# A graph layer's finished rows: two columns of edges written by SP row by row instead of by two indirect DMAs of GpSimd

## What is computed

```python
proj = einsum('ni,rio->nro', x, relation_weight)      # 10 relations
att  = sum(proj[src, etype] * tanh(proj[dst, etype] + efeat), -1)
a    = softmax of att over the edges of one dst
h_nb = segment_sum(x[src] * a[:, None], dst)
out  = leaky_relu((x + h_nb) @ W1.T, 0.01) + leaky_relu((x * h_nb) @ W2.T, 0.01)
result = layernorm(x + out)                            # over the 64 features
```

## Time and profile before

| | us |
|---|---|
| median of 3 runs (lowest to highest) | 926.07 (923.43 to 927.35) |
| span of the profiled execution, first to last instruction | 764.9 |
| rest of the median: what lies around the span | 161.2 |

### The profile page before, as it was taken

The page is one execution under the profiler, slowest core; times in us unless marked ns, Lnnn a source line. Parts: engine busy times, 40 slices in busy tenths (PEclk is TensorE's granted clock), DMA queues, the critical chain, the costliest instruction groups (busy, mean ns, idle before and its releaser), DMA issues. The chain is left out here.

```text
span 764.9 us, 14665 instructions
## 1 busy us (share of the span) xinstructions
PE 556.2 (73%) x3780; PEld 293.9 (38%) x3780; DVE 634.8 (83%) x1115; ACT 499.1 (65%) x1474; POOL 581.8 (76%) x590
## 2 busy tenths in 40 slices
PE   1887888888789788888889887788888788632000
PEld 0652454445345345345345343333333333321000
DVE  1689999999999999999999999999999899742010
ACT  0366677679778779779778777765656446755040
POOL 6777777777777777777777777777777777777776
PEclk9999999999999999999999999999999999755555
DMA  5463435434434434434444332422112221000000
GB/s 134 105 191 81 124 89 144 124 87 145 124 95 137 125 106 126 133 106 117 138 107 115 104 104 73 108 73 75 48 46 74 75 83 44 28 26 17 19 18 16
DMA packets 49457, 70.41 MB, mean 92 GB/s; under 512 B 17450, under 2 KB 20966, under 8 KB 49374
## 3 DMA queue, kind: packets, MB, share of 16 engines
q1 hardware_dynamic: 30750, 52.33, 21.2%
q0 software_dynamic: 18624, 17.16, 10.9%
HBM read 45.61 MB, written 25.78 MB: 93 GB/s over the span
## 5 line engine op out<-in xcount | busy, mean ns | idle before, releaser
L441 POOL DMA_INDIRECT xsd<-in_x,ends_i x384 | 378.2, 985 | 118.0 <-issue 108.6
L543 PE MATMUL t_ps<-xm,w_rel 64*64 64x512 f32 (+1 forms) x1000 | 270.3, 622 | 39.7 <-DVE xm L912 39.2
L912 DVE SCALAR_TENSOR_TENSOR xm<-typ,xT_ps 128x1024 f32<-128x1024 f32 (+1 forms) x250 | 292.4, 1187 | 2.6 <-issue 2.6
L545 PE MATMUL h_ps<-xm,w_rel 64*64 64x512 f32 (+1 forms) x1000 | 270.2, 622 | 0.0
L465 POOL DMA_INDIRECT out<-out_r,row_i x196 | 200.6, 1023 | 59.7 <-issue 55.5
L560 PE MATMUL y_ps<-bd_cat,dT 128*128 128x256 f32 x392 | 97.9, 394 | 17.6 <-DVE zd L974 14.8
L691 ACT ACTIVATE o_t<-zd,rstd 128x64 f32<-128x64 f32 x392 | 98.8, 337 | 14.9 <-DVE rstd L996 14.9
L543 PEld LDWEIGHTS t_ps<-xm,w_rel 64*64 64x64 f32 x1000 | 52.7, 135 | 142.7 <-DVE xm L912 117.4
L578 PE MATMUL s_ps<-bd_both,uwT 128*128 128x128 f32 x392 | 73.4, 313 | 36.6 <-issue 35.9
L578 PEld LDWEIGHTS s_ps<-bd_both,uwT 128*128 128x128 f32 x392 | 54.9, 203 | 115.1 <-issue 95.3
L560 PEld LDWEIGHTS y_ps<-bd_cat,dT 128*128 128x128 f32 x392 | 72.5, 195 | 30.9 <-issue 12.8
(11 more groups left out here) (143 smaller groups left out, 742.1 us busy)
## 6 DMA issues: line engine op xcount, KB each, us to landing
xsd<-in_x SPq DMA_DIRECT2D x1024, 0.2 KB
x_in<-in_x SPq DMA_DIRECT2D x48, 256.0 KB
typ<-typ_d SPq DMA_DIRECT2D x24, 512.0 KB
out<-o_t SPq DMA_DIRECT2D x48, 256.0 KB
xsd<-in_x,ends_i POOLq DMA_INDIRECT x384
hist<-es SPq DMA_DIRECT2D x24, 256.0 KB, 2.0
ea<-in_edge_attr SPq DMA_DIRECT2D x24, 224.0 KB
out<-out_r,row_i POOLq DMA_INDIRECT x196, 2.1
```

The lines of the kernel that those rows point to most:

```text
L441: pool.indirect_dma_start(xsd[:, s % RX, j, side, :], None, x[:, :], bass.IndirectOffsetOnAxis(ap=ends_i[:, side, c:c + 1], axis=0),).then ...
L543: pe.matmul(t_ps[h * D:(h + 1) * D, 0:n], w_rel[0:D, r, :], xm[0:D, b, h * n:(h + 1) * n], start=(r == 0), stop=(r == R - 1), skip_group_c ...
L545: mm = pe.matmul(h_ps[(1 - h) * D:(2 - h) * D, 0:n], w_rel[D:P, r, :], xm[D:P, b, (1 - h) * n:(2 - h) * n], start=False, stop=(r == R - 1) ...
L912: v.scalar_tensor_tensor(xm[:, (s * R + r) % RM, 0:n], typ[:, s % RT, 0:n], float(r), xT_ps[:, 0:n], ALU.is_equal, ALU.mult).then_inc(mask ...
```

## The change

The finished rows of the last column of blocks 14 and 16 are no longer scattered by POOL. SP writes them row by row, 16 chunks of 16 rows, three chunks at the end of each step from s = 23 on, behind the hist store. The addresses are made by DVE in rows() (two 128 x 1 multiplications of a column of `row_i` by 256) and turned into two partitions of `out_ids` by two small DMAs in SP's step 4. A row whose address lies beyond the end is skipped by the DMA's bounds check. The first chunk waits for all dense stores, the first of a block for its rows (`fmul_done`). POOL waits at its very end for the 256 row writes. Beside this `row_ids` becomes one partition for each of the eight columns, in place of one partition for all.

```diff
+    OUT_BLOCKS, OUT_CHUNK, OUT_FROM = [14, 16], 16, 23
...
+        out_at = sb("out_at", [P, len(OUT_BLOCKS)], I32)
+        out_ids = sb("out_ids", [len(OUT_BLOCKS), P], I32)
-        row_ids = sb("row_ids", [1, len(ROW_BLOCKS), P], I32)
+        row_ids = sb("row_ids", [len(ROW_BLOCKS), P], I32)
...
+            out_bytes = out.rearrange("n f -> (n f)").bitcast(U8)
+
+            def load_out_ids():
+                sp.wait_ge(out_at_done, 1)
+                for k in range(len(OUT_BLOCKS)):
+                    sp.dma_start(out_ids[k:k + 1, :], out_at[:, k:k + 1], allow_slow_non_contiguous=True).then_inc(out_ids_in, DMA)
+
+            def rows_to(n):
+                k, part = divmod(n, P // OUT_CHUNK)
+                if not 0 <= n < len(OUT_BLOCKS) * (P // OUT_CHUNK):
+                    return
+                s, j = OUT_BLOCKS[k], cols(OUT_BLOCKS[k]) - 1
+                if n == 0:
+                    sp.wait_ge(out_ids_in, len(OUT_BLOCKS) * DMA)
+                    for m in range(RO):
+                        sp.wait_ge(o_stored[m], o_need(m))
+                if part == 0:
+                    sp.wait_ge(fmul_done, s + 1)
+                p0 = part * OUT_CHUNK
+                ids = [sp.alloc_register(f"to{n}_{i}") for i in range(OUT_CHUNK)]
+                sp.load(ids, out_ids[k:k + 1, p0:p0 + OUT_CHUNK])
+                for i in range(OUT_CHUNK):
+                    at = sp.snap(ids[i], donate=True, min_val=0, max_val=(N - 1) * ROW)
+                    sp.dma_start(out_bytes[bass.DynSlice(at, ROW)].rearrange("(a c) -> a c", a=1),
+                                 out_r[p0 + i:p0 + i + 1, s % RW, j, :].bitcast(U8), bounds_check='skip_entire_dma').then_inc(rows_out, DMA)
...
+                if s == 4:
+                    load_out_ids()
                 if 0 <= s - 1 < NS:
                     store_hist(s - 1)
+                for n in range(3):
+                    rows_to((s - OUT_FROM) * 3 + n)
...
             def scatter(s):
                 pool.wait_ge(fmul_done, s + 1)
-                for j in range(cols(s)):
+                for j in range(cols(s) - (s in OUT_BLOCKS)):
...
+            pool.wait_ge(rows_out, len(OUT_BLOCKS) * P * DMA)
...
+                for k, s in enumerate(OUT_BLOCKS):
+                    c = s * COLS + cols(s) - 1
+                    ins = v.tensor_scalar(out_at[:, k:k + 1], row_i[:, c:c + 1], float(4 * D), None, ALU.mult)
+                ins.then_inc(out_at_done, 1)
...
-                    v.tensor_scalar(row_ids[:, :, :], row_ids[:, :, :], float(4 * D), None, ALU.mult).then_inc(at_done, 1)
+                    v.tensor_scalar(row_ids[:, :], row_ids[:, :], float(4 * D), None, ALU.mult).then_inc(at_done, 1)
```

More of the change, by code:

```diff
@@ L191, in gnn_resnorm @@
         at_done = sem("at_done")
+        out_at_done, out_ids_in, rows_out = sem("out_at_done"), sem("out_ids_in"), sem("rows_out")
         typ_in = sems("typ_in", RT)
@@ L359, in load_ids @@
                 every = dst[0:(P - 1) * T].rearrange("(p c) -> c p", c=T)
-                sp.dma_start(row_ids[0:1, k, 0:P - 1], every[c:c + 1, :], allow_slow_non_contiguous=True).then_inc(ids_in, DMA)
+                sp.dma_start(row_ids[k:k + 1, 0:P - 1], every[c:c + 1, :], allow_slow_non_contiguous=True).then_inc(ids_in, DMA)
                 last = (P - 1) * T + c if c < LASTC else c - LASTC
-                sp.dma_start(row_ids[0:1, k, P - 1:P], dst[last:last + 1].rearrange("(a c) -> a c", a=1)).then_inc(ids_in, DMA)
+                sp.dma_start(row_ids[k:k + 1, P - 1:P], dst[last:last + 1].rearrange("(a c) -> a c", a=1)).then_inc(ids_in, DMA)
             def rows_at(n):
@@ L373, in rows_at @@
                 ids = [sp.alloc_register(f"id{n}_{i}") for i in range(CHUNK)]
-                sp.load(ids, row_ids[0:1, k, p0:p0 + CHUNK])
+                sp.load(ids, row_ids[k:k + 1, p0:p0 + CHUNK])
                 for i in range(CHUNK):
@@ L485, in _ @@
             for k in range(RW):
-                pool.wait_ge(scattered[k], sum(cols(s) for s in range(k, NS, RW)) * DMA)
+                pool.wait_ge(scattered[k], sum(cols(s) - (s in OUT_BLOCKS) for s in range(k, NS, RW)) * DMA)
             pool.wait_ge(fix_out, DMA)
+            pool.wait_ge(rows_out, len(OUT_BLOCKS) * P * DMA)
         @block.tensor
```

## The result

The changed kernel is slower: 963.1 us (median of 4, 960.5 to 968.7) against 924.75 us, a ratio of 1.042 with a 95% interval of 1.039 to 1.045. That is 38 us more, where I forecast 2.55 less and gave "SP becomes the bound" 0.14.

A forecast was written before the change was run, and what follows sets the result against it. The prediction took POOL's list of indirect DMAs, back to back, as the bound. Terms: -2.55 us (two scatters) + 0 + 0 gave span 762.3, time 923.5 us with 161.2 around the span; range 920.8 to 931.

The forecast's parts named there:

- SP becomes the bound: At the program's end: SP's last row write is issued after POOL's last scatter; 936 us at 0.42 a row; chance 0.14.
- The time around the span: Whole program: median 926.07 us against a profiled span of 764.9, so 161.2 us lie outside it, carried over unchanged.
- the first step: Whole program: POOL's indirect DMAs, back to back, first gathers and then scatters, are the time of the kernel.
- The cover: Program's end: POOL's last 80 or so scatters cover SP's 256 row writes, with 10 us to spare; term 0.
- I take 0.33: SP's single-row writes: 0.33 us a row, like the plain row read, between 0.33 or less and 0.46.
- The gain of two scatters: POOL's scatter list: two scatters fewer at 1.27 us each, all on the path; term -2.55 us.
- The preparation: Addresses on DVE and SP's two loads at step 4: DVE gains 0.3 us, SP at most 3 us, hidden; term 0.
- The check: Bounds check on SP's row writes: its price is in no row; taken within 0.33 us a row, less for dropped rows.
- the first rival: "SP becomes the bound": end at 667.4 + 256d, d the cost of a row; POOL's wait on rows_out ends the program; chance 0.14.
- The rival of serial landing: SP's row writes each hold the DMA engine until landed: 512 us for 256, time about 1,318 us; chance 0.02.
- The rule of the Trainium skill: SP's 256 small writes: coalescing advice spoke against the change; to worsen the sum only if the 10 us cover is gone.

The follow-up runs named there:

- the repeated kernel before: The kernel before, unedited, run again for a profile beside its own time: 917.9 us with a span of 916.1.
- SP's part alone: Changed kernel, but POOL scatters all 196 columns and SP writes the 256 rows to a DRAM tensor of its own: 952.1 us against 915.7, ratio 1.040.
- no check: Changed kernel with all 256 rows written to a DRAM tensor of its own, without bounds check: 976.2 us against 923.6 before, ratio 1.056.
- one step earlier: Changed kernel with the row writes from step 22 in place of 23: 954.0 us against 923.6 before, ratio 1.029.
- eight at a time: Changed kernel with the numbers loaded in 32 loads of eight in place of 16 of sixteen: 962.5 us against 923.6 before, ratio 1.042.

## Why the prediction was wrong

**The time around the span.** The step that failed first is "so 161.2 us lie around the span; I carry them over unchanged". The runs show 1.8 us around it. The rest is inside the timed executions, and it changes both terms that decided whether SP was covered. It also takes away the first step, that POOL's list is the time of the kernel: POOL waits for PE and ACT.

**The cover.** I had POOL's last scatter end 117 us after SP comes free behind store_hist(22) (641.5 to 758.8). In the changed kernel it is 834.5 to 927.6, 93 us. In the trace that I had, POOL was behind the compute and had 88 scatters left when hist(22) went out, back to back to the end. In the changed kernel it had kept pace with the slower compute and had 51 left, with 24.6 us of waits (above 0.5 us each) between them. From the first scatter of block 20 on both take about as long, 47 and 52 us; what shrank is the stretch before it.

**"I take 0.33" for a row.** The single instruction was priced right, the write as the read (0.227 against 0.228 us, MOVE 0.029), and the load as well (1.23 for my 1.35). The sum over 256 rows wasn't: 16 x 1.35 + 256 x 0.33 = 106 us, 106.9 with the two hist stores, were 129.4. SP pauses between and inside these instructions, and the same pauses stand in the repeated kernel before. With every row written, 106.9 us were 143.0, so the pauses cost 36 us there; in the changed kernel the 83 dropped rows give some 12 back. Sum of both misses: 24.2 + 22.5 = 46.7 us; my 10.4 us to spare became 36.3 us too late. That is the loss: 963.9 less 927.6 us in the trace, 38 us in the medians, 36 in those of SP's part alone, where SP ends 31.3 us behind POOL.

**The gain of two scatters.** "All of it is on the path" was wrong. In the repeated kernel before POOL waits for PE's marks in most blocks and 11.0 us for ACT in front of block 20's scatters, so what is saved on blocks 14 and 16 turns into waits. Only a part of them is seen: with eight scatters fewer, 4.2 us for PE at block 15 and 11.6 for ACT at block 20; with two fewer the wait at block 20 stays 11.0. Two and eight scatters fewer give the same 0.4%. Where these 0.4% come from no run shows.

**What held.** The preparation costs nothing (0.999). The check costs nothing that shows. The mechanism of the first rival was what happened, with its place, the wait on rows_out; its formula asked for the cost of a row alone and held the start and POOL's end fixed, while both moved. The rival of serial landing is refuted for writes: without the check 130 go out in 53.25 us, 0.41 each, loads among them, and the span ends 3 us behind the last, where a landing takes 2.0 us. The rule of the Trainium skill that I weighed ("DMA: Bandwidth & Descriptors", section "Rules for kernel authors": coalesce many small transfers) pointed the right way: a scatter of 128 rows costs POOL 1.27 us, the same rows here cost SP 65 us, and nothing covered the last 36.

## What to carry to other kernels

Compare the span of a profile with the times before anything else: if they differ by more than a few us, the profile is of another execution, and each margin in it has to be doubted, above all one of 10 us that is to hide 100 us of issuing. Work moved to another engine's list is free only as long as that list has room, waits in it or an end before the last engine's: one block's rows fitted before POOL's end and cost nothing (1.002), two blocks' rows didn't. With the single-row gathers gone SP had 299 us of waits in the main loop, and there the same row writes cost nothing. The better kernel is the one before without single rows on SP: 0.978.

## What was not expected of the hardware

In every trace but the one with the span of 764.9 us, SP's instructions stop again and again with no wait that the profile shows: a MOVE of 29 ns takes up to 1,132 ns and a DMA issue of 228 ns up to 1,400 in the repeated kernel before, against at most 38 and 323 ns. Others are recorded with 2 ns, so only sums over many of them should be read. Six chunks of single-row reads took this long in one step of the changed kernel and of the repeated kernel before, where the earlier trace rows has 20.12 us:

```profile
644.11 42.30 SPq L381 DMA_DIRECT2D xsd<-in_x  x48
```

```profile
622.34 48.17 SPq L377 DMA_DIRECT2D xsd<-in_x  x48
```

POOL's scatters mostly keep their 0.97 and 0.30 us in the same stretch, apart from their waits. And the pauses end with POOL's list. In the changed kernel POOL's last instruction ends at 927.6 us, and behind 933.6 us every MOVE of the writes takes 29 ns:

```profile
L407 SPq MOVE out<-out_r x80: 29/29/29, 934.8 to 963.8; - x80
```

In four other runs with row writes that go on behind POOL's end (SP's part alone, no check, one step earlier, eight at a time) the last MOVE above 200 ns starts between 1.0 us before and 2.3 us behind it. The trace without pauses has the same list of POOL, so that list alone isn't their cause. What makes SP pause, and why one execution had none of it, no run shows; recording the trace may have a part in it, and there is no execution without a recording to tell. Nor is it shown how much of the slower main loop the pauses make: PE was busy 67.7 us longer in the repeated kernel than in the trace that I had (623.9 and 556.2), at a mean granted clock of 0.843 and 0.917, and no run tells whether that is a cause or follows from its waits. That fewer SP instructions make the kernel faster fits the pauses, but doesn't name them.
